# Taking the next image's group statistics earlier in an attention loop, from a second read of the image

## The reference, cut to what matters

```python
def _gn(v, G=32, eps=1e-5):
    B_, C_, H_, W_ = v.shape
    g = v.reshape(B_, G, C_ // G, H_, W_)
    m = jnp.mean(g, axis=(2, 3, 4), keepdims=True)
    s = jnp.var(g, axis=(2, 3, 4), keepdims=True)
    return ((g - m) / jnp.sqrt(s + eps)).reshape(v.shape)

# layer 0: attention over the 1024 pixels, 8 heads of 64
xs = x.reshape(b, c, seq).transpose(0, 2, 1)
qkv = xs @ Wqkv + bqkv
scores = jnp.einsum('bhqd,bhkd->bhqk', q, k) / jnp.sqrt(...)
attn = jax.nn.softmax(scores, axis=-1)
out = jnp.einsum('bhqk,bhkd->bhqd', attn, v)
x = x + _L0_conv_ref(_gn(x), ...)
# layer 1: 16 windows of 8x8 pixels; a small convolution gives 4 sample points
# per window and group, keys and values are sampled there, a two-layer MLP on
# the logarithm of the distances gives a bias for the similarities
x = x + _L1_conv_ref(_gn(x), ...)
```

## Time and profile before

| | us |
|---|---|
| median of 3 runs | 3103.03 (3098.18 to 3104.87) |
| the profiled execution, time | 3095.78 |
| its span in the trace | 3094.0 |
| PE busy | 2826.2 (91% of the span) |
| DVE busy | 2207.2 (71%) |
| ACT busy | 1657.7 (54%) |
| PE idle before L642, released by ACT's exponentials L1069 | 49.2 |
| PE idle before L660, released by DVE's copy L1398 | 38.7 |
| PE idle before L701, released by DVE L1345 | 18.7 |
| PE idle before L715, released by DVE's low half L1360 | 18.4 |
| DVE statistics of the pixels, L1335 on `x_image` | 40.1 (64 of 681 ns) |

### The profile page before, as it was taken

One profiled execution on the slowest core, in us unless ns is written; L12 is line 12 of the kernel. 1 busy time (PEld: TensorE's weight loads), 2 busy tenths in 40 slices (PEclk: granted clock), 3 DMA queues, 4 the chain that ended last, 5 costly groups with the idle time before them and its releaser, 6 DMA issues.

```text
span 3094.0 us, 59663 instructions
## 1 busy us (share of the span) xinstructions
PE 2826.2 (91%) x24696; PEld 1964.6 (63%) x24696; DVE 2207.2 (71%) x2934; ACT 1657.7 (54%) x2429; POOL 197.0 (6%) x157
## 2 busy tenths in 40 slices
PE   6999799999999999899999999999998999998858
PEld 5666576756766577665776667665676756765434
DVE  5666677687775787767867777668777587775746
ACT  2563465374663755535654556536465375663624
POOL 0000020000200002000020001100020000200200
PEclk9999899999999999999999999999999999998968
DMA  5123013311134011340123211332113311104040
GB/s 196 51 59 110 28 33 90 116 58 52 37 80 165 6 54 37 102 145 28 37 62 119 93 42 32 64 123 79 44 38 86 121 51 52 37 12 169 14 105 28
DMA packets 141534, 221.10 MB, mean 71 GB/s; under 512 B 77713, under 2 KB 96660, under 8 KB 137396
## 3 DMA queue, kind: packets, MB, share of 16 engines
q1 hardware_dynamic: 136596, 190.03, 19.8%
q10 hardware_dynamic: 4672, 27.26, 3.6%
HBM read 162.40 MB, written 54.84 MB: 70 GB/s over the span
## 4 chain that ended last, share of the span: by engine, by line
PE 71%; DVE 16%; issue 4%; DMA 3%; ACT 3%; SPq 1%; another core or an unknown queue 0%; ACTq 0%; DVEq 0%; POOL 0%
PE banks L673 12%; PE banks L613 10%; PE banks L642 9%; PE banks L660 8%; PE banks L603 6%; PE banks L852 5%; PE banks L715 4%; PE banks L862 3%; DVE neg_max L1389 3%; PE banks L853 3%; PE banks L854 3%; DVE exps_turned L1398 3%; DMA point_outputs_dram<-point_outputs 2%; PE banks L825 2%; DVE qk_halves L1567 1%
## 5 line engine op out<-in xcount | busy, mean ns | idle before, releaser
L1389 DVE TENSOR_REDUCE neg_max<-banks 128x1 f32<-128x1024 f32 x512 | 601.4, 1216 | 91.1 <-PE banks L642 90.3
L1069 ACT ACTIVATE exps<-banks,neg_max 128x1024 f32<-128x1024 f32 x512 | 566.6, 1113 | 46.7 <-DVE neg_max L1389 46.5
L1079 ACT ACTIVATE exps_turned<-banks 128x1024 f32<-128x1024 f32 x256 | 262.3, 1025 | 579.8 <-PE banks L660 569.4
L1398 DVE COPY exps_turned<-banks 128x1024 f32<-128x1024 f32 x256 | 313.1, 1223 | 324.7 <-PE banks L660 310.5
L642 PE MATMUL banks<-qk_halves 64*128 64x512 f32 x3072 | 440.3, 418 | 72.1 <-ACT exps L1069 49.2
L673 PE MATMUL banks<-exps_turned,values 128*64 128x256 f32 x4096 | 480.0, 384 | 0.8 <-issue 0.8
L660 PEld LDWEIGHTS banks<-ident,exps 64*128 64x128 f32 x8192 | 312.1, 140 | 215.4 <-issue 190.1
L660 PE MATMUL banks<-ident,exps 64*128 64x64 f32 x8192 | 367.4, 229 | 43.8 <-DVE exps_turned L1398 38.7
L642 PEld LDWEIGHTS banks<-qk_halves 64*128 64x128 f32 x3072 | 296.9, 192 | 124.4 <-issue 88.7
L673 PEld LDWEIGHTS banks<-exps_turned,values 128*64 128x64 f32 x4096 | 279.7, 137 | 138.3 <-issue 4.0
L1567 DVE SCALAR_TENSOR_TENSOR qk_halves<-banks,qk_halves 128x1024 fp32r<-128x1024 f32 x256 | 301.6, 1217 | 85.6 <-ACT qk_halves L1118 85.4
(11 more groups left out here) (181 smaller groups left out, 3344.2 us busy)
## 6 DMA issues: line engine op xcount, KB each, us to landing
wqk_ring<-wqk_split SPq DMA_DIRECT2D x62, 512.0 KB, 4.3
wo_halves<-wo_split_dram SPq DMA_DIRECT2D x8, 2048.0 KB, 7.6
exps_turned<-in_x SPq DMA_DIRECT2D x32, 512.0 KB, 5.5
x_dram<-exps SPq DMA_DIRECT2D x32, 512.0 KB, 2.6
exps_turned<-x_dram SPq DMA_DIRECT2D x32, 512.0 KB, 6.2
out<-exps_turned SPq DMA_DIRECT2D x32, 512.0 KB, 2.8
recips_b<-recips_dram SPq DMA_DIRECT2D x240, 64.0 KB, 3.5
x_image<-in_x ACTq DMA_DIRECT2D x14, 1024.0 KB, 14.2
```

What stands on the lines that cost most here:

```text
L1069: freed(act.activation(PB[:, 2 * h + n % 2], slot(("s", m, i)), ACT.Exp, bias=NM[:, m:m + 1], accum_out=SS[:, m:m + 1]), ("s", m, i))
L1389: dve.tensor_reduce(NM[:, m:m + 1], slot(("s", m, i)), AX.X, ALU.max, negate=True).then_inc(mx, 1)
L1398: dve.tensor_copy(PT[:, n // 2 % 2, 1, :, P * j:P * j + P].rearrange("p k (r q) -> p k r q", r=2), TB.rearrange("p r (k q) -> p k r q", k= ...
```

## The change

The statistics of image `i+1` are no longer taken from `X`. The sync engine reads the image a second time, as eight pieces of 128 channels by 512 pixels (256 KB each), into two buffers of 512 numbers per partition that share their place with small tensors of layer 1 (`CVS` and `SMB`). It issues two pieces behind the reciprocals of `u` = 2, 4, 6, 8, and DVE takes their statistics in steps 8, 12, 16 and 20 (`sample_stats`, two `bn_stats` each). Channel means come in step 21, group sums and variance in step 22. The whole image is then read into `X` as before, but SP issues it, behind the reciprocals of `u` = 10. DVE normalises tiles 0 and 1 in step 25 and 2 and 3 in step 26; ACT's high halves come in steps 26 and 27, and DVE's low halves one in each of steps 27 to 30. The group sums now lie in the first columns of PE's bank, and the wait that protects them moves from `similarities` to `turn_weights`.

```diff
-        T4 = sb("conv_sums", [P, 256])
-        TG = sb("conv_gelu", [P, CT, 64])
+        CVS = sb("conv_or_sample", [P, 512])
+        T4 = CVS[:, 0:256]
+        TG = CVS[:, 256:512].rearrange("p (t c) -> p t c", t=CT)
...
-        SMP = sb("probabilities", [P, 2, 4, 32])
-        AT2 = sb("probabilities_turned", [P, 4, 64])
+        SMB = sb("probs_or_sample", [P, 512])
+        SMP = SMB[:, 0:256].rearrange("p (h l e) -> p h l e", h=2, l=4)
+        AT2 = SMB[:, 256:512].rearrange("p (c n) -> p c n", c=4)
+        XSAMPLE = (CVS, SMB)
...
+            def next_image(i):
+                wait_full(sp, ("s", 47, i - 1))
+                for h in range(2):
+                    sp.dma_start(X[:, 2 * h:2 * h + 2], x[i].rearrange("(t p) n -> p t n", p=P)[:, 2 * h:2 * h + 2])\
+                        .then_inc(x_in[h], 16)
+
+            def load_sample(c, k):
+                wait_after(sp, xs_done, 8 * (k - 1) + c - 1)
+                if c == 1:
+                    wait_after(sp, o1_full, 2 * (k - 2))
+                sp.dma_start(XSAMPLE[c % 2][:], x[k, P * (c // 2):P * (c // 2) + P, 512 * (c % 2):512 * (c % 2) + 512])\
+                    .then_inc(xs_in[c % 2], 16)
+
             for i in range(B):
                 for u in range(OUTS - 1):
                     recips_around(u, i)
+                    if i + 1 < B and u in (2, 4, 6, 8):
+                        load_sample(u - 2, i + 1)
+                        load_sample(u - 1, i + 1)
                     if u == 6 and i:
                         rows_to_dram(i - 1)
                     if u == 2 and not i:
                     if u in (1, 3, 5, 7):
                         load_wq(4 + u // 2, i)
                     if i + 1 < B:
+                        if u == 10:
+                            next_image(i + 1)
                         if u in (9, 11):
                             load_wq(u // 2 - 4, i + 1)
...
                 if j + 1 < B:
                     pe.wait_ge(piece_free, (j + 2) * MAXES)
+                if j + 2 < B:
+                    pe.wait_ge(gn_var, 2 * j + 4)
...
                 pe.wait_ge(kz_done, j + 1)
-                if f == 0 and j + 2 < B:
-                    pe.wait_ge(gn_var, 2 * j + 4)
...
-                    if i + 1 < B and n == 26:
-                        group_sums(2 * i + 2, GSO)
+                    if i + 1 < B and n == 22:
+                        pe.wait_ge(piece_free, (i + 1) * MAXES)
+                        group_sums(2 * i + 2, GSM)
...
-            def next_image(i):
-                wait_full(act, ("s", 47, i - 1))
-                for h in range(2):
-                    act.dma_start(X[:, 2 * h:2 * h + 2], x[i].rearrange("(t p) n -> p t n", p=P)[:, 2 * h:2 * h + 2])\
-                        .then_inc(x_in[h], 16)
...
-                    if i + 1 < B and n == 22:
-                        next_image(i + 1)
...
-                    if i + 1 < B and n in (27, 28):
-                        x_high(2 * (n - 27), i + 1)
-                        x_high(2 * (n - 27) + 1, i + 1)
+                    if i + 1 < B and n in (26, 27):
+                        x_high(2 * (n - 26), i + 1)
+                        x_high(2 * (n - 26) + 1, i + 1)
...
+            def sample_stats(c, k):
+                dve.wait_ge(xs_in[c % 2], 64 * (k - 1) + 16 * (c // 2 + 1))
+                dve.bn_stats(BNS[:, c // 2, c % 2], XSAMPLE[c % 2][:]).then_inc(xs_done, 1)
+
             def group_channels(last):
                 link(last)
+                channel_means()
+
+            def channel_means():
                 dve.memset(PAUSE[:], 0.0)
...
-                    if i + 1 < B and n == 28:
-                        x_low(0, i + 1)
...
                     if i + 1 < B:
-                        if n == 24:
+                        if n in (8, 12, 16, 20):
+                            sample_stats((n - 8) // 2, i + 1)
+                            sample_stats((n - 6) // 2, i + 1)
+                        if n == 21:
+                            dve.wait_ge(xs_done, 8 * (i + 1))
+                            channel_means()
+                        if n == 25:
                             dve.wait_ge(x_in[0], 16 * (i + 1))
-                            group_parts(X, 0)
-                            group_parts(X, 1)
-                        if n == 25:
-                            dve.wait_ge(x_in[1], 16 * (i + 1))
-                            group_parts(X, 2)
-                        if n == 26:
-                            group_channels(group_parts(X, 3))
-                        if n == 27:
                             dve.wait_ge(gn_rstd, 2 * i + 2)
                             normalise(0)
                             normalise(1)
-                        if n == 28:
+                        if n == 26:
+                            dve.wait_ge(x_in[1], 16 * (i + 1))
                             normalise(2)
                             normalise(3)
-                        if n == 29:
-                            x_low(1, i + 1)
-                        if n == 30:
-                            x_low(3, i + 1)
+                        if 27 <= n < 31:
+                            x_low(n - 27, i + 1)
                     if n % 2:
                         if n < STEPS - 1:
                             recips(n // 2, i)
...
-                    if i + 1 < B and n == 26:
-                        group_variance(2 * i + 2, GSO)
+                    if i + 1 < B and n == 22:
+                        group_variance(2 * i + 2, GSM)
                     if i and n == 26:
                         key_blocks(i - 1)
-                    if i + 1 < B and n == 29:
-                        x_low(2, i + 1)
```

9 lines of the change are left out of this document (5 added, 4 removed).

## The result

The changed kernel takes 3058.49 us (median of 4 runs, 3052.57 to 3060.57), the kernel before 3102.02 (4 runs on the same chip). Two later comparisons of the same kernel gave 0.9895 (0.9876 to 0.9914) and 0.9856 (0.9822 to 0.9890), that is 30.8 and 51.0 us between the medians. The sign and the mechanism held, the size didn't.

A forecast was written before the change was run, and what follows sets the result against it. PE was taken to bound steps 12 to 21; in 22 to 30 PE and DVE wait in turns. Gains 22.8 + 3.0 + 5.0 less costs 2 and 1 give 28 us: median 3075, range 3061 to 3092.

The forecast's parts named there:

- Steps 24 and 25: Image 3, 14.1 us before: without the four statistics the copy of step 24 ends sooner; 1.1 less, new 13.0.
- Step 26: Image 3, 8.4 us before: group sums and their wait go, the copy comes 0.24 later; 1.1 less, new 7.3.
- Steps 27 to 29: Image 3, 18.8 us before: exponentials, similarities and ACT's ring decide, not DVE; 18.7, nothing gained.
- Step 30: Image 3, 7.2 us before: the low half behind step 29's copy goes, values start at 6.1; 1.1 less.
- I take half, 5.0 (bounds 0 and 10.5): Images 1, 4, 5, 6, 10.5 us above image 3 in sum: issues leave ACT, slow spells may return; 5.0 gained.
- The costs: Added time: 2 us for step 12's statistics and logarithm copy near POOL, 1 us for image 0 waiting on tiles.
- A: Steps 22 to 30: moved work was hidden anyway, only two plain DVE waits go; 3090 us, chance 0.12.
- B: Step 12: POOL blocks the statistics and delays the logarithms, 2.7 us per image; 3089 us, chance 0.06.
- D: Steps 8 to 21: no slack, late pieces stop DVE and then PE, 7 us per image; 3124 us, chance 0.05.
- C: Image stretch: all steps fall to the ring, no slow spells return, 42 us gained; 3061 us, chance 0.08.
- the ring: Steps 23 to 30: score matmuls, transposition, ACT's copy and two exponentials that free the banks; fastest step 5.55 us.
- nothing is due: Reciprocals of u = 11, behind the image, 5 to 7 us later: output scaled 28 us after computing, so no wait.

The follow-up runs named there:

- the old tail: Changed kernel with early statistics kept, but normalisation and high halves back in steps 27 and 28, low halves in 28 to 30: 3063.18 us, ratio 0.9883.
- with the additions: Kernel before plus only the second image read and its eight statistics in steps 8, 12, 16, 20, results unused: 3100.08 us, ratio 0.9999.
- with six more: Kernel before plus six small DMAs issued by ACT in step 6 of image 0: 3095.68 us, one run.
- third execution: Changed kernel unaltered, measured a third time beside the later experiments: 3057.23 us, ratio 0.9856 to the kernel before.
- the repeat: Changed kernel unaltered, measured a second time beside more runs of the kernel before: 3067.99 us, ratio 0.9895.

## Why the prediction was wrong

**The mechanism held, in its steps.** Steps 24 and 25: 13.0 forecast, 12.7 measured. Step 26: 7.3 and 7.4. Steps 27 to 29: 18.7 and 18.3. Step 30: 6.1 and 6.1. The whole stretch: 56.25 and 55.7. Image 0: 3.0 and 3.2 off. Per image 1 to 6 I had 3.8; images 2 and 3 gained 4.5 and 4.4. At image 3's 4.4 that makes 26.4, 3.6 more than forecast. The split inside is not as I put it: by the run with the old tail, the early statistics and SP's issue bring 4.1 of the 4.4 (the issue alone 0.3). Of these, 1.4 come in steps 24 and 25 and 2.0 in step 26, for which I had 1.1 each, and 0.5 in step 27, for which I had nothing. The tail's 1.1 in step 30 is nearly given back by the normalisations that it moves into steps 25 and 26, so booking 1.1 for it was right for the step and wrong for the sum.

**The step that failed** is the term "I take half, 5.0 (bounds 0 and 10.5)". It was the excess of images 1, 4, 5 and 6 over image 3. I had written the price of the issue as 0.4 us an image and the slow spells as something that may come again elsewhere. The long issue on ACT is no chance of one execution: one of 3.1 to 3.6 us stood in images 5 and 6 in each of the four kernels in which ACT issues two DMAs in a row (before, with the additions, with six more, and the changed kernel with the issue on ACT), and ACT had none in any other. It takes 2.3 to 2.7 us longer than the ordinary one itself and, with the slow matmuls behind it, costs 4.3 and 4.9 us before the change (SP issues: 72.9 to 68.6, 74.7 to 69.8), and 5.1 and 4.5 in steps 22 and 23 after it. Over all, the excess of the four images fell from 11.7 us (image 5's window in the earlier trace rows begins 1.2 late: its score matmuls start at 1981.3) to 1.6, so 10.1 and not 5.0. Nearly all of it is images 5 and 6. My caution was not empty, though: the changed kernel's third execution was as clean as the first (506.2 us of stretches), but in the repeat stops and slow spells came in other images and took 13.8 us back. That repeat is also the comparison with the smallest gain; the kernel before wasn't profiled beside it, so how often either kernel has such spells stays open.

**The costs** of 3.0 did not show: with the additions alone steps 8 to 21 took 609.2 us for 610.2, and image 0 didn't wait for its successor's tiles (the 0.4 us on `x_image` in all is for the first image of the launch). Sum of what came out in the stretches: 26.4 + 3.2 + 10.1 = 39.7 (39.5 in the table), for which I had 22.8 + 3.0 + 5.0 - 3.0. Of the 12 us between, 5.1 are the slow images, 3.6 the step sum and 3.0 the costs.

**The median** moved by 43.5, 7 more than the profiled executions, and no row says where these 7 are. Three comparisons of the same pair gave 30.8, 43.5 and 51.0. The forecast of 28 lies under all three medians, though inside the interval of the lowest (27 to 38 us by the ratio). The 0.2% that I called the resolution of a measurement, 6 us, was too small: the comparisons lie 0.4% apart.

**The rivals.** A (the moved work was hidden anyway) is refuted by the step lengths. B (statistics held by POOL) by 0.69 and 0.68 us in step 12 and the ratio 0.9999. D (no slack in the early steps) by the same ratio; its place was real, though: in the changed kernel DVE waited four times for a piece, 6.9 us in all. Behind the longest, 3.6 us, step 21 of image 5 took 8.2 us for 5.7, and in the third execution one of 3.7 goes with a step 13 of 10.2 us. With the pieces asked for one output earlier no such wait or one of 1.3 us was left, so the late asking is what made them, as far as two executions show. C comes nearest: the slow spells of images 5 and 6 did not return, and each image gave 0.6 us more. Its other half failed: only steps 23 and 29 fell to the ring's 5.6 us, the others stayed at 5.7 to 7.4. I gave it 0.08, and the traces didn't bear out so little: a 3.63 us issue in a row that I quoted was a cause with a name, which the change removes.

**Small readings.** A DMA share of 0.19 means that the engines were idle four fifths of that time, not two thirds. And "nothing is due" was wrong for the reciprocals of u = 11: in the run with the old tail DVE waited 2.77 us for them in image 6, and PE behind it.

**What the two rules of the Trainium skill did.** The Trainium skill, "SBUF — State Buffer", "Who interferes with whom", lets a DVE instruction with at most one SBUF input, outside the two-port modes, pass GpSimd freely. The trace agrees for the statistics (675 to 693 ns beside POOL, 675 to 694 without).

The Trainium skill, "DMA: Bandwidth & Descriptors", "Queues, rings and completion order", has each DMA engine take one queue in order and several in turns. From it I had the image landing sooner in one queue with the reciprocals, and they later. The landing did fall, from a median of 14.2 us to 6.9 (5.2 to 13.6), but the shared queue isn't the reason. In the kernel that issues the image on SP right behind the write of the reciprocals, before it has landed, both are in one queue too, and the image took 13.8 us (11.0 to 20.1). What the quick landings have in common is that the write of u = 10 was done before the image was asked for.

The reciprocals did come later. In image 3 SP's round from write to read-back took 12.0 us for u = 11 and 14.9 for u = 12, for 10.9 and 11.5 before. DVE waited for reciprocals four times, 7.4 us in all, which it never did before the change; in step 31 it was for u = 13:

```profile
1289.74 0.42 DVE L1441 TENSOR_TENSOR attended<-attended,recips_b 128x256 f32<-128x256 f32 x1 [2.87 <-DMA recips_b<-recips_dram]
```

That wait isn't on the path: PE's values ran through. It isn't the image's place alone either: with the image on SP but the old, longer steps DVE waited 0.2 us, and with ACT issuing but the short steps 2.0. That points to the shorter steps, which leave SP's round less time.

## What to carry to other kernels

Ask of a row that stands out in one or two repetitions of a loop whether the change removes its cause; if it does, book all of it, with the slow matmuls behind it, and not half. In these runs two issues in a row held their engine for 3 us in some repetitions and 0.9 in others, so large transfers are better issued by an engine that doesn't compute. Moving work off a busy stretch pays what stands on the chain there (DVE lost 5.4 us of work here, an image 4.1), and moving work within it paid nearly nothing (0.3). When several transfers share one engine's queue, each one moved forward pushes another back: look at who waits for that one.

## What the runs showed of the hardware

- Two DMAs of 1 MB issued in a row took ACT 0.90 us in images 0 to 4 and 3.1 to 3.6 in images 5 and 6, in four executions of four kernels. With 2.3 us between them each took at most 0.74 (one execution). One of 2 MB took 0.37 to 0.43.
- On SP the pair took 1.10 us in most images and up to 3.1 in the changed kernel; SP's issues of the small read-backs of reciprocals show the same now and then (3.11 for 1.10).
- The image's 1 MB transfers landed in 6.9 us (median) from SP's queue when the write of the reciprocals before them had landed, in 13.8 from the same queue when it hadn't, and in 14.2 from ACT's queue beside that write. As one DMA of 2 MB in ACT's queue the image took 18.3.
- A `bn_stats` of 128x512 took 0.68 us, beside POOL's `tensor_tensor` as without it; a bf16 copy of 64x512 took 1.50 in step 13 and 0.39 in step 12 beside it, and 0.28 or 0.41 without.
- PE and ACT stop now and then for 2 to 5 us with no wait that the trace shows (4.17 us in PE, with the value weights landing; 4.74 in ACT, with the image landing); behind PE's stop the mean granted clock was 0.67 of 2.4 GHz for 8 us. No cause for it was tested.
